# Attention scores of the first two groups from the split parts, 32 rows at a time, and a new order of the first loads and preparations

## The chip, the core and the metric

One core of a Trainium2 chip. A core has five engines with queues of their own: PE (matrix multiplies, into the eight PSUM banks), DVE (vector), ACT (activations), POOL (GpSimd) and SP (used here to issue DMAs). They run side by side and wait for each other by semaphores. The metric is the device time of one execution in microseconds (us), the median of the runs shown.

## What is computed

A transformer block on 2048 rows of 512 numbers: cross attention with a residual, then a layer with a shared feed-forward net and eight experts.

```python
attn = einsum('bhdq,bhdk->bhqk', q, k)          # q = layernorm(x), k = v = ctx, heads of 32 channels
out  = einsum('bhqk,bhdk->bhdq', softmax(s * attn), v)
x = x + out
# on layernorm(x): out = top-2 of 8 experts (gelu, rank-32 side path) + 0.2 * shared net
x = x + moe(layernorm(x))
```

The heads lie along the 128 rows of a group: a group has 4 heads of 32 rows, and 16 groups make 2048 rows. A score matrix of one head is 512 x 512.

## The kernel before

The function `work_order` writes one list of units by hand, `plan`; every engine walks through this list and issues its own part of each unit, in that order. So the place of a unit in the list sets the order on all engines at once, and a wait in one unit holds all that stands behind it on that engine.

Group g goes through these units. **load** g (SP): x rows to `xin` and context rows to `cin` (four and two buffers). **prepare** g: `stats`, `aggr`, `rstd` (layer norm; DVE, with a power of one column on POOL between, L719), `norm` (DVE L1002), `x_hi`, `x_lo`, `c_lo` (DVE L1008, L1012, L1017, and ACT L811 for the context): the normed rows and the context rows, each as a bf16 high part and a bf16 rest, in `split[g % 2]` (four parts). **bounce** g (SP): the four parts go to DRAM (`split_parts`) and come back as stacks `QS` and `KS`: six DMAs, so that one head's three products hi*hi, lo*hi and hi*lo become one contraction over 96 rows. **score** g, i (16 units: head h, 128 query rows t): one matmul of 96 rows and 512 columns (PE L1335) into a PSUM bank, and DVE takes the row maximum (L1038). **parts**, **rows**, **row**: the negative maxima are turned by PE (L1349) and laid by ACT (L830, four copies) into rows 96 and 97 of `QS`; the matching rows of `KS` are set to one by POOL (unit `fills`, L727). **exp** g, i: a matmul of the stacks, 128 rows (PE L1365), and ACT's exponential (L840). **values** g, t, k: four fp32 matmuls side by side in column strips of 32 (PE L1384), once for the sums and once for the values, the latter from `VT`, which `turn_v` makes by turning `cin` (PE L1317, ACT L825). Then `den`, `attn`, `resid` (DVE L1055 to L1064), a second layer norm (`stats2` to `norm2`, with a POOL step `rstd2`, L723), `x2_hi`, `x2_lo`, `turn`, `gate`, `xt_lo`.

Beside this the weights of the shared net come in: `w_load` 0 to 7 (SP L628, 1 MB each), `w_split` n: ACT makes the bf16 high part of a quarter (L856), and POOL subtracts it in four pieces (L743) for the low part. `wd` and `wu` are small side weights.

After the first two groups (window 0) the kernel runs windows of two groups: `open_window(w)` ends the group before, `scores_and_up(w)` mixes the scores of group 2w+1 with the 16 `up` steps of the shared net (12 matmuls of 256 columns each, PE L1428), `exponentials_and_down(w)` mixes the exponentials with the `down` steps. Seven such windows follow window 0, then the routing and the experts. The change touches window 0 and the first two functions of window 1.

In the first stretch the list is: `load` 0 and 1, `small`, `w_load` 0, `prepare` 0 with its bounce, `w_load` 1, `prepare` 1, `fills`, `w_load` 2 to 7, then the 16 scores of group 0, with `load` 2 and 3 placed among them, behind all weight loads on SP's queue.

Of the kernel before, what the change touches and what calls it, by code (L numbers as in the profile page):

```python
# [4 lines left out]

# [9 lines left out]
P = 128  # L15
# [19 lines left out]
STACK = 6  # L35
# [17 lines left out]
def work_order():  # L53
# [98 lines left out]
    def open_window(w):  # L152
# [20 lines left out]
        if w < WINDOWS:  # L173
            add("turn_v", 2 * w + 1)
            add("load", 2 * w + 2) if 2 * w + 2 < GROUPS else None
# [10 lines left out]
        if w < WINDOWS:  # L186
            add("parts", 2 * w)
            if 2 * w + 3 < GROUPS:
                add("load", 2 * w + 3)

    def scores_and_up(w):
        a = 2 * w
        score = scores((a + 1) * UNITS, (a + 2) * UNITS)
        rows = max_rows(a)
        for n, _ in enumerate(shared_up(w - 1)):
            if n >= 3:
                next(rows, None)
            next(score, None)
        for _ in score:
            pass  # L200
        add("parts", a + 1)

    def exponentials_and_down(w):
        downs = [shared_down(w - 1, 0)] if w else []
        for k, g in enumerate((2 * w, 2 * w + 1)):
            score = iter(())
            if k == 1:
                side = [average(g - 1), norm2(g - 1), rows2(g - 1)]
            elif w < WINDOWS - 1:
                side = [prepare(n) for n in (g + 2, g + 3)]  # L210
                if w == 0:
                    score = scores(UNITS, 2 * UNITS)
            else:
                side = []
            values = []
            rows = max_rows(g + 1)
            for i in range(UNITS):
# [4 lines left out]
                if w == 0 and k * UNITS + i in (2, 14, 18, 22, 26):  # L222
                    add("w_split", 3 + (2, 14, 18, 22, 26).index(k * UNITS + i))
                if i >= 4 * k:
                    one_of(side, 3 if k and i < 6 else 2)
# [27 lines left out]
    add("load", 0)  # L253
    add("load", 1)
    add("small")
    add("w_load", 0)
    for _ in prepare(0):
        pass
    add("w_load", 1)
    for _ in prepare(1):  # L260
        pass
    add("fills")
    for k in range(2, 8):
        add("w_load", k)
    add("rank_load")
    add("w_split", 0)
    for i, _ in enumerate(scores(0, UNITS)):
        if i in (0, 4):
            add("turn_v", i // 4)
        if i in (6, 12):  # L270
            add("load", 1 + i // 6)
        if i in (2, 8):
            add("w_split", 1 + i // 8)
    add("scales")
    add("parts", 0)
    for _ in max_rows(0):
        pass
    early, placed = [], []
    exponentials_and_down(0)
    add("wd", E)  # L280
    for w in range(1, WINDOWS):
        open_window(w)
        if w == 1:
            add("b2_parts")
            add("wu", E)
        scores_and_up(w)
# [66 lines left out]
def build(nc, x, ctx_in, itok, gate_w, w1, b1, w2, b2, wd, wu, sw1, sb1, sw2, sb2, swd, swu, out):  # L353
    stack = ExitStack()
    with stack:
# [226 lines left out]
        def sync_program(sp):  # L582
            dma = nc.sync.dma_start
            for unit in plan:
                kind = unit[0]
                if kind == "load":
# [5 lines left out]
                    dma(xin[g % NX][:, :], x_rows[rows, :]).then_inc(s_x[g % NX], 16)  # L592
                    if g >= 2:
# [11 lines left out]
                elif kind == "bounce":  # L605
# [11 lines left out]
                    for dst, parts in ((QS[s], (0, 1, 0)), (KS[s], (2, 2, 3))):  # L617
                        if g == 0 and dst is KS[0]:
                            continue
# [77 lines left out]
        def pool_program(pool):  # L697
# [16 lines left out]
            for unit in plan:  # L714
# [9 lines left out]
                elif kind == "fills":  # L724
                    pool.wait_ge(s_clo, 2)
                    for i in range(NS):
                        gp.memset(KS[i][96:P, :, :], 1.0).then_inc(s_fills, 1)  # L727
                        pool.wait_ge(s_fills, i + 1)
                    gp.memset(wus[96:P, :], 0.0).then_inc(s_fills, 1)
# [4 lines left out]
                elif kind == "w_split":  # L734
                    n = unit[1]
# [6 lines left out]
                    for a in range(4):  # L742
                        gp.tensor_tensor(lo[:, a], whole[:, a], hi[:, a], ALU.subtract).then_inc(s_wlog, 1)  # L743
# [58 lines left out]
        def act_program(act):  # L802
            act.wait_ge(s_pool, CONSTANTS)
            for unit in plan:
                kind = unit[0]
                if kind == "x_hi":
                    g = unit[1]
                    if g >= 2:
                        act.wait_ge(s_stack[(g - 2) % NS], 16 * STACK * ((g - 2) // NS + 1))
                    act.wait_ge(s_c[g % 2], 16 * (g // 2 + 1))  # L810
                    ac.activation(split[g % 2][:, 2, :], cin[g % 2][:, :], ACT.Copy).then_inc(s_khi, 1)  # L811
                elif kind == "bounce" and unit[1] == 0:
                    act.wait_ge(s_parts, 16)
                    for k, which in enumerate((2, 2, 3)):
                        ac.dma_start(KS[0][HD * k:HD * k + HD, :, :],
                                     parts_dram[0, which].rearrange("(h p) c -> p h c", p=HD)).then_inc(s_stack[0], 16)
                elif kind == "fills":
# [152 lines left out]
        def dve_program(dve):  # L970
# [9 lines left out]
            for unit in plan:  # L980
# [22 lines left out]
                elif kind == "x_hi":  # L1003
                    g = unit[1]
                    if g >= 2:
                        dve.wait_ge(s_stack[(g - 2) % NS], 16 * STACK * ((g - 2) // NS + 1))
                    dve.wait_ge(s_dve, chain)
# [10 lines left out]
                elif kind == "fills":  # L1018
# [245 lines left out]
        def pe_program(pe):  # L1264
# [38 lines left out]
            for unit in plan:  # L1303
                kind = unit[0]
                if kind == "fills":
# [13 lines left out]
                elif kind == "score":  # L1319
# [3 lines left out]
                    if i == 0:  # L1323
# [6 lines left out]
                    if was:  # L1330
# [4 lines left out]
                    mm(bank(score_bank[unit]), QS[s][0:96, h, t * P:t * P + P], KS[s][0:96, h, :],  # L1335
                       start=True, stop=True).then_inc(s_score, 1)
# [15 lines left out]
                elif kind == "exp":  # L1352
# [5 lines left out]
                    if i == 0:  # L1358
                        pe.wait_ge(s_row, GH * (g + 1))
# [245 lines left out]
```

## Time and profile before

| | us |
|---|---|
| median of 3 runs (1519.56 to 1521.75) | 1519.76 |
| the profiled execution | 1527.68 |
| its span, first to last instruction | 1525.9 |
| first score matmul | 17.56 |
| rows of maxima of group 0 / group 1 on PE | 31.93 / 67.59 |
| first `rank` matmul (the shared net begins) | 113.75 |
| last `up` matmul of window 1 | 142.6 |
| each later window | 82.61 |

The page's first part gives busy time by engine: PE 1417.7 (93% of the span), DVE 779.3 (51%), ACT 695.8 (46%), POOL 222.0 (15%). Over the whole span PE is the engine that is nearly always busy; the first 100 us are the exception. What a stage is limited by is read from that stage's own rows: which engine sits idle there, and what ended its idle time.

### The profile page before, as it was taken

Reading aid. Unit: us, or ns where it says so; the run is one execution under the profiler, and the core shown is the slowest. Engines: PE = TensorE matmul, PEld = TensorE weight load, DVE = VectorE, ACT = ScalarE, POOL = GpSimd, SP = SyncE. Lnnn points to the kernel's source line nnn. Section 1 sums busy time; section 2 is a strip of 40 time slices with the busy share of each in tenths; the row PEclk is TensorE's granted clock in tenths of the full one; section 3 lists DMA queues with packets and bytes.
Section 4 is the critical chain, followed back from the end, with each engine's and each line's share of the span. In section 5 each row is a group of like instructions: output and inputs, shape, how many; then the busy total and the mean of one; then the engine's idle time right before and its main releaser. Section 6 shows DMA issues by size and latency. Waiting matters only on the chain.

```text
span 1525.9 us, 27002 instructions
## 1 busy us (share of the span) xinstructions
PE 1417.7 (93%) x11297; PEld 1001.1 (66%) x11368; DVE 779.3 (51%) x1287; ACT 695.8 (46%) x1015; POOL 222.0 (15%) x219
## 2 busy tenths in 40 slices
PE   3569999999999999988999999999999999999996
PEld 1126372726354453626588888998888888888884
DVE  5477565756574756726462552625436264352620
ACT  4546456464737373743443434534344343443411
POOL 6240000000000000053300201203021120210202
PEclk8779999999999999999999999999999999999998
DMA  8410213122222212202832543526345262441402
GB/s 271 152 55 15 77 49 90 50 83 56 74 66 70 70 49 56 78 15 29 284 111 85 144 111 113 144 85 178 92 130 128 85 170 85 132 130 65 91 6 35
DMA packets 93211, 145.41 MB, mean 95 GB/s; under 512 B 15529, under 2 KB 36153, under 8 KB 93090
## 3 DMA queue, kind: packets, MB, share of 16 engines
q1 hardware_dynamic: 80370, 118.08, 23.5%
q0 software_dynamic: 12288, 25.21, 9.6%
q8 instruction: 90, 1.47, 0.4%
q10 hardware_dynamic: 432, 0.39, 0.1%
q14 instruction: 31, 0.25, 0.1%
HBM read 109.47 MB, written 34.15 MB: 94 GB/s over the span
## 4 chain that ended last, share of the span: by engine, by line
PE 78%; issue 11%; DVE 4%; ACT 2%; DMA 1%; POOL 1%; SPq 1%; another core or an unknown queue 0%; POOLq 0%; ACTq 0%; DVEq 0%
PE banks L1545 23%; PE banks L1520 23%; PE banks L1428 11%; PE banks L1445 7%; PE banks L1384 3%; PE banks L1335 3%; PE banks L1508 2%; PE banks L1365 1%; PE banks L1482 1%; PE banks L1560 1%; PE banks L1404 1%; DVE rowmax L1038 1%; DMA split_parts<-hidden 1%; DMA xin<-in_x 1%; ACT hidden L840 1%
## 5 line engine op out<-in xcount | busy, mean ns | idle before, releaser
L1545 PE MATMUL banks<-hidden,w2h 128*128 128x0 bf16 x2048 | 324.5, 276 | 0.0
L1545 PEld LDWEIGHTS banks<-hidden,w2h 128*128 128x128 bf16 x2048 | 198.3, 98 | 29.3
L840 ACT ACTIVATE hidden<-banks,scales 128x512 f32<-128x512 f32 x256 | 163.4, 684 | 109.5 <-PE banks L1365 86.7
L1545 PE MATMUL banks<-hidden,w2l 128*128 128x0 bf16 x1024 | 198.5, 275 | 0.0
L1038 DVE TENSOR_REDUCE rowmax<-banks 128x1 f32<-128x512 f32 x256 | 170.4, 680 | 43.8 <-PE banks L1335 43.1
L929 ACT ACTIVATE hf<-banks,b1cols 128x640 f32<-128x640 f32 x128 | 101.5, 793 | 181.5 <-PE banks L1520 178.9
L1445 PE MATMUL banks<-w2h,hidden 128*128 128x512 bf16 x499 | 176.3, 382 | 1.0 <-issue 0.2
L1164 DVE TENSOR_TENSOR w1l<-stage,w1h 128x2048 bf16<-128x2048 f32 x32 | 73.3, 2292 | 193.5 <-ACT w1h L905 193.5
L1335 PE MATMUL banks<-KS,QS 96*128 96x512 bf16 x256 | 100.8, 403 | 38.1 <-DVE rowmax L1038 27.2
L1520 PE MATMUL banks<-eth,w1l 128*128 128x0 bf16 x1024 | 135.9, 276 | 0.0
L1520 PE MATMUL banks<-eth,w1h 128*128 128x0 bf16 x1024 | 135.9, 276 | 0.0
L1520 PE MATMUL banks<-etl,w1h 128*128 128x0 bf16 x1024 | 135.9, 276 | 0.0
L935 ACT ACTIVATE yT<-banks 128x640 f32<-128x640 f32 x32 | 22.5, 703 | 195.9 <-PE banks L1545 195.9
L1365 PEld LDWEIGHTS banks<-QS,KS 128*128 128x128 bf16 x256 | 20.6, 98 | 136.7 <-ACT hidden L840 83.3
L1520 PEld LDWEIGHTS banks<-eth,w1l 128*128 128x128 bf16 x1024 | 99.8, 98 | 15.2
L1545 PEld LDWEIGHTS banks<-hidden,w2l 128*128 128x128 bf16 x1024 | 99.9, 98 | 15.2
L1520 PEld LDWEIGHTS banks<-etl,w1h 128*128 128x128 bf16 x1024 | 99.8, 97 | 15.2
L1365 PE MATMUL banks<-QS,KS 128*128 128x512 bf16 x224 | 81.3, 397 | 30.5 <-ACT hidden L840 18.7
L1520 PEld LDWEIGHTS banks<-eth,w1h 128*128 128x128 bf16 x1024 | 99.9, 98 | 14.7
L1155 DVE CAST hidden<-hf 128x640 bf16<-128x640 f32 x128 | 62.9, 492 | 88.7 <-ACT hf L929 88.5
L1157 DVE TENSOR_TENSOR hidden<-hf,hidden 128x640 bf16<-128x640 f32 x128 | 105.6, 825 | 4.4
L1055 DVE RECIPROCAL rden<-banks 128x128 f32<-128x128 f32 x64 | 55.1, 914 | 95.4 <-PE banks L1384 67.2
(176 smaller groups left out, 2025.5 us busy)
## 6 DMA issues: line engine op xcount, KB each, us to landing
stage<-in_L_ffn_w SPq DMA_DIRECT2D x64, 1024.0 KB
split_parts<-hidden SPq DMA_DIRECT2D x16, 512.0 KB, 3.0
QS<-split_parts SPq DMA_DIRECT2D x48, 128.0 KB, 2.5
KS<-split_parts SPq DMA_DIRECT2D x45, 128.0 KB, 2.7
xin<-in_x SPq DMA_DIRECT2D x16, 256.0 KB, 2.8
cin<-in_ctx SPq DMA_DIRECT2D x16, 256.0 KB, 2.9
out_rows<-xin SPq DMA_DIRECT2D x16, 256.0 KB, 2.0
normed_rows<-x2r SPq DMA_DIRECT2D x16, 256.0 KB, 2.0
```

The lines of the kernel that those rows point to most:

```text
L840: ac.activation(prob[n % NPH], bank(score_bank[unit]), ACT.Exp, scale=scales[:, g // 2:g // 2 + 1]).then_inc(s_exp, 1)
L929: ac.activation(by_half(hf[n % 2][:, :]), PB[:, b0:b0 + 2, 0:CAP].rearrange("p j (c r) -> p j c r", r=HP), ACT.Gelu, bias=b1cols[:, e * FB ...
L1038: dv.reduce_max(rowmax[g % 2][:, i:i + 1], bank(score_bank[unit]), X_AXIS).then_inc(s_max, 1)
L1155: link(dv.tensor_copy(hh[:, fb, :], hf[n % 2][:, :]))
L1157: dv.tensor_tensor(hl[:, fb, :], hf[n % 2][:, :], hh[:, fb, :], ALU.subtract).then_inc(s_hl, 1)
L1164: dv.tensor_tensor(lo, stage[j % NST][:, :].rearrange("p (a w) -> p a w", w=512), hi, ALU.subtract).then_inc(s_wlo, 1)
L1335: mm(bank(score_bank[unit]), QS[s][0:96, h, t * P:t * P + P], KS[s][0:96, h, :], start=True, stop=True).then_inc(s_score, 1)
L1365: mm(bank(score_bank[unit]), KS[s][:, h, t * P:t * P + P], QS[s][:, h, :], start=True, stop=True).then_inc(s_st, 1)
L1428: issued = mm(bank(b)[:, 0:PASS], weights[:, kb, f0:f0 + P], data[:, kb, :], start=n == 1, stop=n == 3 * KB)
L1445: issued = mm(bank(b_down), a[:, fb, cols], w[:, fb, :], start=False, stop=(fb, k) == (FB - 1, 2))
L1520: issued = mm(half_of(bank(b0 + j)).shape_from_register(bank_cols(e, j)), weights[:, kb, f0:f0 + P], half_of(data[:, kb, :], j).shape_from ...
L1545: issued = mm(half_of(bank(b0 + j)).shape_from_register(bank_cols(e, j)), w[:, fb, rows], half_of(a[:, fb, :], j).shape_from_register(slot ...
```

## The change

- Scores of groups 0 and 1 no longer use the stacks. Each is three matmuls of 32 rows (hi*hi, lo*hi, hi*lo) that add up in one bank, read straight from `split[g]` at the head's own rows 32h to 32h+31. They wait for `x_lo` and `c_lo` of the group in place of the six stack DMAs, and run head by head in turn. The stacks are still made, for the exponentials.
- `load` is parted in `load` (x) and `c_load` (context). x 2 and 3 are loaded at the start; context 2 after `w_load` 2, context 3 before `w_load` 5.
- `prepare` 1 stands behind the scores of group 0, `prepare` 3 in the exponentials of group 1. All six stack DMAs of group 0 are on SP (three were on ACT). `split` of groups 2 and 3 may be written only when the scores of groups 0 and 1 are done.
- `w_split` keeps ACT's part; POOL's four pieces are units of their own, `w_lo`, strewn among the following units. `fills` is in two parts: `KS` 0 and 1 early, the rest behind the last piece.
- In window 1, the last eight scores of group 2 move from `open_window` to the first `up` steps; `b2_parts` and `wu` move behind `up` 8. An `exp` waits for its own head's row copy.

```diff
     def scores(first, last):
         for n in range(first, last):
-            add("score", n // UNITS, n % UNITS)
+            g, i = divmod(n, UNITS)
+            add("score", g, i % GH * QT + i // GH if g < 2 else i)
             yield
...
         score = scores(2 * w * UNITS + EARLY, (2 * w + 1) * UNITS) if w < WINDOWS else iter(())
+        late = score if w == 1 else iter(())
+        if w == 1:
+            score = iter(())
...
         for n, _ in enumerate(shared_up(w - 1)):
-            if n >= 3:
+            if n >= (6 if w == 1 else 3):
                 next(rows, None)
             next(score, None)
+            if w == 1 and n < 8:
+                next(score, None)
+            if w == 1 and n == 9:
+                add("b2_parts")
+                add("wu", E)
...
                 side = [average(g - 1), norm2(g - 1), rows2(g - 1)]
+                if w == 0:
+                    side.insert(0, prepare(g + 2))
...
-                if w == 0 and k * UNITS + i in (2, 14, 18, 22, 26):
-                    add("w_split", 3 + (2, 14, 18, 22, 26).index(k * UNITS + i))
+                if w == 0 and k * UNITS + i in (4, 12, 20, 28):
+                    n = 3 + (4, 12, 20, 28).index(k * UNITS + i)
+                    split_quarter(n)
+                else:
+                    low_piece()
...
+    for g in range(2):
+        add("load", g)
+        add("c_load", g)
+    for g in range(2, 4):
+        add("load", g)
     add("small")
     add("w_load", 0)
...
-    add("w_load", 1)
-    for _ in prepare(1):
+    for k in range(1, 3):
+        add("w_load", k)
+    add("c_load", 2)
+    for k in range(3, 5):
+        add("w_load", k)
+    add("turn_v", 0)
+    add("turn_v", 1)
+    for i, _ in enumerate(scores(0, UNITS)):
+        if i == 4:
+            add("fills", 0)
+        if i in (6, 10, 14):
+            split_quarter(i // 4 - 1)
+        else:
+            low_piece()
+    add("parts", 0)
+    rows = max_rows(0)
+    for _ in second:
+        next(rows, None)
+        low_piece()
+    for _ in rows:
         pass
+    add("scales")
+    add("rank_load")
+    add("c_load", 3)
+    for k in range(5, 8):
+        add("w_load", k)
...
-    add("wd", E)
+    split_quarter(7)
+    while pieces:
+        low_piece()
+    add("fills", 1)
...
-                    if i == 0:
+                    if i == 0 and g < 2:
+                        pe.wait_ge(s_xlo, g + 1)
+                        pe.wait_ge(s_clo, g + 1)
+                    elif i == 0:
                         pe.wait_ge(s_stack[s], 16 * STACK * (g // NS + 1))
...
+                    if g < 2:
+
+                        rows = slice(HD * h, HD * h + HD)
+                        for k, (q, c) in enumerate(((0, 2), (1, 2), (0, 3))):
+                            issued = mm(bank(score_bank[unit]), split[g][rows, q, t * P:t * P + P], split[g][rows, c, :],
+                                        start=k == 0, stop=k == 2)
+                        issued.then_inc(s_score, 1)
...
-                    if i == 0:
-                        pe.wait_ge(s_row, GH * (g + 1))
+                    if i == 0 and g < 2:
+                        pe.wait_ge(s_stack[s], 16 * STACK)
+                    if t == 0:
+                        pe.wait_ge(s_row, GH * g + h + 1)
```

PE at the end of the scores of group 0 and the first exponentials. Before (L1335 a score, L1349 the rows, L1365 an exp):

```order
L1335 MATMUL banks<-KS_65,QS_61 128x512 x11
L1349 MATMUL banks<-identb,MS 32x128 x16
L1365 MATMUL banks<-QS_61,KS_65 128x512
L1335 MATMUL banks<-KS_66,QS_62 128x512
L1365 MATMUL banks<-QS_61,KS_65 128x512
```

Now (L1397 a score of 32 rows, L1415 the rows, L1433 an exp):

```order
L1397 MATMUL banks<-hidden 128x512 x2
L1415 MATMUL banks<-identb,MS_74 32x128 [waits s_vtc,s_ms]
L1415 MATMUL banks<-identb,MS_74 32x128 x15
L1433 MATMUL banks<-QS0_61,KS0_65 128x512 [waits s_row,s_max,s_stack0,s_fills]
L1397 MATMUL banks<-hidden 128x512 [waits s_max,s_clo,s_xlo]
L1397 MATMUL banks<-hidden 128x512 x2
L1433 MATMUL banks<-QS0_61,KS0_65 128x512 [waits s_max,s_row]
```

Each matmul of a score has become three of 32 rows, and the first of group 1 waits for `prepare` 1 itself.

POOL from its first power (the layer norm's `rstd`) to the second layer norm of group 1. Before (L719 `rstd`, L727 `fills`, L743 low pieces, L723 `rstd2`):

```order
L719 TENSOR_TENSOR mv<-mv,half 128x1 x2
L727 MEMSET KS_65 32x2048
L743 TENSOR_TENSOR w1l<-w2h,w1h 128x512 x8
L743 TENSOR_TENSOR w1l<-w2l,w1h 128x512 x4
L719 TENSOR_TENSOR mv<-mv,half 128x1
...
L743 TENSOR_TENSOR w2l<-hidden,w2h 128x512 x8
L723 TENSOR_TENSOR mv<-mv,half 128x1
L743 TENSOR_TENSOR w2l<-late_stage,w2h 128x512 x4
L723 TENSOR_TENSOR mv<-mv,half 128x1
```

Now (L773 `rstd`, L781 `fills`, L798 low pieces, L777 `rstd2`):

```order
L773 TENSOR_TENSOR mv<-mv,half 128x1
L781 MEMSET KS_65 32x2048
L781 MEMSET KS_66 32x2048
L798 TENSOR_TENSOR w1l<-w2h,w1h 128x512 x8
L798 TENSOR_TENSOR w1l<-w2l,w1h 128x512
L773 TENSOR_TENSOR mv<-mv,half 128x1
...
L798 TENSOR_TENSOR w2l<-hidden,w2h 128x512 x2
L777 TENSOR_TENSOR mv<-mv,half 128x1
L798 TENSOR_TENSOR w2l<-hidden,w2h 128x512 x6
L798 TENSOR_TENSOR w2l<-late_stage,w2h 128x512 x4
L781 MEMSET KS_67 32x2048
```

The `rstd` of group 1 now stands behind nine low pieces, the `rstd2` of group 0 behind two pieces of its quarters in place of eight, and that of group 1 behind the late `fills`.

SP, the issue of loads around the weights. Before:

```order
L632 DMA wuf<-in_L_ffn_swu 32x512 x3
L592 DMA xin_56<-in_x 128x512
L597 DMA cin_58<-in_ctx 128x512
L592 DMA xin_57<-in_x 128x512
L597 DMA cin_59<-in_ctx 128x512
```

Now:

```order
L653 DMA cin_59<-in_ctx 128x512
L645 DMA xin_56<-in_x 128x512
L645 DMA xin_57<-in_x 128x512
L655 DMA scale_i<-in_itok_B_1933 128x8
...
L682 DMA w2l<-in_L_ffn_sw 128x4x512
L653 DMA cin_58<-in_ctx 128x512
L682 DMA w2l<-in_L_ffn_sw 128x4x512
```

x 2 and 3 (`xin_56`, `xin_57`) have moved from behind all weight loads to the front, and context 2 stands between two of them.

## Rows read from the trace of the kernel before

**Rows 1.** Busy time by stage: us, PE, PEld, DVE, ACT, POOL busy (instructions), PEclk, DMA share, GB/s.

```profile
0.00:17.56 17.56, 0.66 (x2) 0.36 (x3) 6.67 (x15) 5.83 (x6) 6.15 (x17) 1.00 0.77 220
17.56:31.93 14.37, 8.35 (x25) 3.56 (x25) 12.97 (x21) 3.67 (x4) 14.00 (x14) 0.77 0.84 284
31.93:48.75 16.82, 3.94 (x23) 1.09 (x24) 2.20 (x6) 9.81 (x12) 5.46 (x5) 0.60 0.96 329
48.75:67.59 18.84, 15.47 (x71) 3.19 (x73) 16.43 (x28) 9.12 (x13) 6.38 (x6) 0.80 0.33 105
67.59:99.35 31.76, 20.90 (x120) 4.01 (x122) 16.66 (x27) 18.67 (x25) 19.67 (x17) 0.79 0.12 38
99.35:113.75 14.40, 8.37 (x42) 6.41 (x39) 12.35 (x23) 3.67 (x5) 0.66 (x1) 0.66 0.30 95
113.75:142.60 28.85, 28.65 (x238) 23.11 (x237) 21.00 (x43) 16.06 (x35) 0.00 (x0) 0.93 0.03 8
150.17:232.78 82.61, 79.00 (x553) 41.09 (x559) 51.20 (x98) 46.54 (x84) 4.33 (x6) 1.00 0.23 66
```

**Rows 2.** Chain of work that ended last, first 152 us: start, length, what.

```profile
7.78 3.99 DMA split_parts<-hidden
...
39.41 7.77 DMA xin<-in_x
...
77.15 4.52 POOL w2l L743 x4
81.69 4.89 POOL w2l L743 x4
...
122.91 1.31 PE banks L1428 x12
```

**Rows 3.** Timeline, matmuls: start, length of the merged piece, engine, line, operation, count.

```profile
17.96 1.06 PE L1317 MATMUL banks<-ident,cin 128*128 128x128 f32 x4
18.81 1.91 PE L1335 MATMUL banks<-KS,QS 96*128 96x512 bf16 x4
...
61.39 0.38 PE L1335 MATMUL banks<-KS,QS 96*128 96x512 bf16 x1
61.70 1.07 PE L1384 MATMUL banks<-hidden,VT 128*32 128x512 f32 x8
62.70 0.39 PE L1365 MATMUL banks<-QS,KS 128*128 128x512 bf16 x1
...
72.08 1.94 PE L1384 MATMUL banks<-hidden,ones_f 128*32 128x512 f32 x8
...
90.44 0.10 PEld L1335 LDWEIGHTS banks<-KS,QS 96*128 96x128 bf16 x1 [6.32 <-DVE rowmax L1038]
```

**Rows 4.** Timeline of ACT, POOL and SP; in brackets the idle time before and its releaser.

```profile
14.58 7.37 POOL L727 MEMSET KS<- 32x2048 bf16 x4 [5.24 <-DVE hidden L1017]
22.05 1.27 SPq L621 DMA_DIRECT2D QS<-split_parts  x3
23.98 8.93 POOL L743 TENSOR_TENSOR w1l<-w2h,w1h 128x512 bf16<-128x512 f32 x8
31.25 1.91 ACT L856 ACTIVATE w1h<-w2l 128x2048 bf16<-128x2048 f32 x1 [8.18 <-DMA w2l<-in_L_ffn_sw]
33.18 2.42 ACT L830 ACTIVATE QS<-banks 32x512 bf16<-32x512 f32 x4
```

**Rows 5.** Timeline of DVE.

```profile
19.48 9.23 DVE L1038 TENSOR_REDUCE rowmax<-banks 128x1 f32<-128x512 f32 x15 [0.59 <-PE banks L1335]
50.00 0.78 DVE L1002 TENSOR_SCALAR xn<-xin,mv 128x512 f32<-128x512 f32 x1
53.56 1.64 DVE L1017 TENSOR_TENSOR hidden<-cin,hidden 128x512 bf16<-128x512 f32 x1
```

**Rows 6.** Stretches of 1 us, PE alone: us, PE busy (instructions), PEclk, DMA share, GB/s.

```profile
25.00:26.00 1.00, 0.66 (x2) 0.70 1.01 273
52.00:53.00 1.00, 1.00 (x9) 0.65 0.00 0
```

More of the change, by code:

```diff
@@ L4 @@
 from concourse import mybir
+import itertools
 import numpy as np
@@ L185, in open_window, with scores_and_up, late_scores @@
             pass
[L186 removed]
+        if 1 < w < WINDOWS:
             add("parts", 2 * w)
[L188 to L193 removed]
+        if 2 * w + 3 < GROUPS:
+            add("load", 2 * w + 3)
+            add("c_load", 2 * w + 3)
+        return late
+    def scores_and_up(w, late):
+        a = 2 * w
+        def late_scores():
+            for _ in late:
+                yield
+            if w == 1:
+                add("parts", a)
+        score = itertools.chain(late_scores(), scores((a + 1) * UNITS, (a + 2) * UNITS))
         rows = max_rows(a)
         for n, _ in enumerate(shared_up(w - 1)):
[L196 removed]
+            if n >= (6 if w == 1 else 3):
                 next(rows, None)
             next(score, None)
+            if w == 1 and n < 8:
[3 more added lines that the diff above has]
+                add("wu", E)
         for _ in score:
@@ L251, in beside, with split_quarter, low_piece @@
             yield
-    add("load", 0)
-    add("load", 1)
+    pieces = []
+    def split_quarter(n):
+        add("w_split", n)
+        pieces.extend((n, a) for a in range(4))
+    def low_piece():
+        if pieces:
+            add("w_lo", *pieces.pop(0))
+    for g in range(2):
[3 more added lines that the diff above has]
+        add("load", g)
     add("small")
     add("w_load", 0)
-    for _ in prepare(0):
-        pass
-    add("w_load", 1)
-    for _ in prepare(1):
-        pass
-    add("fills")
-    for k in range(2, 8):
+    first, second = prepare(0), prepare(1)
+    for _ in range(8):
+        next(first)
+    add("k_hi", 1)
+    for _ in first:
+        pass
+    for k in range(1, 3):
[18 more added lines that the diff above has]
+    for _ in rows:
+        pass
+    add("scales")
+    add("rank_load")
+    add("c_load", 3)
+    for k in range(5, 8):
         add("w_load", k)
[L265 to L277, printed above, removed]
     early, placed = [], []
     exponentials_and_down(0)
-    add("wd", E)
+    split_quarter(7)
+    while pieces:
+        low_piece()
+    add("fills", 1)
     for w in range(1, WINDOWS):
[L282 to L286, printed above, removed]
+        scores_and_up(w, open_window(w))
         if w == WINDOWS - 1:
@@ L809, in act_program @@
                         act.wait_ge(s_stack[(g - 2) % NS], 16 * STACK * ((g - 2) // NS + 1))
+                    if g in (2, 3):
+                        act.wait_ge(s_score, UNITS * (g - 1))
                     act.wait_ge(s_c[g % 2], 16 * (g // 2 + 1))
                     ac.activation(split[g % 2][:, 2, :], cin[g % 2][:, :], ACT.Copy).then_inc(s_khi, 1)
[L812 to L817, printed above, removed]
+                elif kind == "fills" and unit[1] == 0:
                     act.wait_ge(s_scale, 1)
```

41 lines of the change are left out of this document (25 added, 16 removed).

## The prediction, made before the changed kernel ran

> **What bounds the kernel now.** I read the stages first [rows 1]. From 150 us on each window takes 82.61 us, PE is busy 79.0 of them at the full clock (1.00, 2.4 GHz), and the change leaves all windows after the first up stage as they are. In the up stage (113.75 to 142.6) PE is busy 28.65 of 28.85 us. So the change can win only before 113.75 us, and may lose in the up stage; what has been won at 142.6 us is the result, since the rest only shifts. Before 113.75 us no engine is full. Then I read the chain [rows 2] for what each stage waits for. Up to 17.56 us: the bounce of group 0, whose write starts at 7.78 and lands 3.99 us later, and the stack reads behind it. Up to 31.93: DVE's row maxima, 9.23 us for 15 [rows 5], 0.62 us each, while a score of 512 columns costs PE 0.22 us at the full clock (twelve matmuls of 256 columns take 1.31 us [rows 2]; the 0.38 in other rows is a modelled length). Up to 48.75: x of group 2, issued at 39.41 behind all weights, landing 7.77 us later; PE is busy 3.94 of 16.82 us. From 67.59 to 113.75: PE is busy 29.3 of 46.2 us; the longest hole is 6.32 us before 90.44 [rows 3], where DVE's second layer norm waits for a power on POOL that stands behind eight low pieces (77.15 and 81.69) [rows 2].
>
> **Step 1: the scores of group 0 start early, and it is worth little.** They need only the four parts, ready at 7.78 us. Both turns of V now stand ahead of them on PE (1.06 us each at the low clock [rows 3], with a copy on ACT between), so the first score starts at about 8.5 us instead of 17.56. Sixteen scores of three matmuls at the full clock are 16 x 0.65 = 10.4 us, DVE's maxima 9.8 us, so with some first scores at the low clock (3 x 0.43 = 1.3 us; pace of 1.91 = 3 x 0.43 + 0.63 [rows 3]) they end near 22 us, 7 us earlier than before. But the next score, the first of group 1, waits on PE for `prepare` 1, and that has gone behind them. Nothing of the 7 us is kept unless `prepare` 1 keeps up.
>
> **Step 2: what `prepare` 1 waits for.** Its `rstd` stands on POOL behind nine low pieces, and the ninth needs `w_split` 2, so `w_load` 2. Two more loads of 256 KB stand ahead of the first bounce: 0.52 MB at 284 GB/s [rows 1] would be 1.8 us; part of it falls in a slack of the queue, I take 1.2, so the write lands at 13.0 instead of 11.77. Before, from the issue of a stack's six DMAs (22.05) to the moment ACT could take the 1 MB weight load behind it (31.25) went 9.2 us [rows 4]. So `w_load` 1 is there at 22.2 us, and `w_load` 2 after another 1.05 MB at 329 GB/s [rows 1], at 25.4. ACT splits each in 1.91 us [rows 4]: 24.1 and 27.3. POOL takes 1.12 us a piece (8.93 for eight): four pieces of quarter 1 end at 28.6, the ninth at 29.7, and with 0.6 allowed for the power of one column DVE goes on at 30.3. That is from `norm` to `c_lo`. Before, for group 2 and beside a busy POOL, that took from 50.00 to 55.20 with two maxima between [rows 5]: 5.2 - 1.24 = 3.9 us. So `c_lo` 1 is ready at 34.2 us. The four row copies of ACT (2.42 [rows 4]) end at about 30 us and are hidden by this; if `prepare` 1 came earlier, they would bound it.
>
> **Step 3: exponentials of group 0 beside scores of group 1.** x of group 2 is long there, so the hole of 7.77 us [rows 2] is gone. But PE now has per pair of exp and score 0.22 + 3 x 0.22 = 0.87 us instead of 0.43, and each pair goes from 128 rows to 32 and back. No row shows such a switch; the nearest is that to column strips: from a score's start to the strips' start 0.31 us instead of 0.22, and from there to the next exp 1.00 us for four passes of 0.22 [rows 3], so 0.09 + 0.14 = 0.23 us for there and back. I take 0.23 from this row; the bounds are 0 and 0.43 (a matmul's whole time, twice). A pair is 1.10 us, sixteen 17.6; five steps of values lie between, 1.09 us each, 5.5. The stage starts at the low clock, as it did at 48.75, where the rise came between 52 and 53 us [rows 1, 6]; the same again loses 2 us. Sum 25.1 us: the last score ends at 59.3. DVE's 16 maxima and one preparation (9.9 + 3.9 us) and ACT's work (9.12 us in this stage before, with a split of 1.91 and an exponential or two more now) lie beside it. Then come one maximum (0.62), the last values step (1.09) and the parts: I allow 1.8 us, so the rows of maxima come at 61.1 instead of 67.59. **Won so far: 6.5 us.**
>
> By the Trainium skill (page TensorEngine Tiling (Array Packing), Key Properties) changing the tiling mode drains TensorE, which speaks against interleaving these two forms. The rows above show the same for column strips, 0.23 us for there and back; by a change without any drain the sum of the stage would be 3.7 us less.
>
> **Step 4: from the rows of group 1 to the shared net (46.2 us before).** Gone: the hole of 6.32 us [rows 3], as the power of group 0 stands behind two pieces now; and five maxima of group 2 between 99.35 and 113.75, where DVE is busy 12.35 of 14.4 us [rows 1], 5 x 0.62 = 3.1. Added: `prepare` 3 on DVE (3.9 us as in step 2, and its statistics), hidden, since DVE idles here (16.66 busy of 31.76 [rows 1]) until the values of group 0 are summed; without this cover it would cost them whole. Part of the hole comes back: POOL's pieces ended at 86.58 [rows 2], so 3.9 us of it, up to 90.44, were DVE's own second norm and casts beside POOL, which stay; one maximum now stands ahead of the casts, so I take 2.7 (bounds 0 and 3.9). New: `fills` and all low pieces stand ahead of the last power (group 1) on POOL: eight pieces of 1.12 from when ACT has split quarter 6, then two memsets of 1.84 (7.37 for four) and the rest of `fills`, 2.0 (from 21.95 to 23.98) [rows 4]; that ends some 4 us after DVE asks for the power, and `norm2`, `turn`, `gate` and the first `rank` are queued behind it. Sum -6.3 - 3.1 + 2.7 + 4.0 = -2.7. **Won so far: 9.2 us**, `rank` at about 104.5 us. The bounds of the POOL wait are 0 (ACT reaches the splits earlier) and 8 (it reaches them 4 us later).
>
> **Step 5: the up stage gets longer.** Before, an up step took 1.31 us [rows 2] and a score of 0.22. Now the first eight steps carry two scores: 0.22 x 8 = 1.8 us more for PE. DVE was busy 21.0 of 28.85 us in this stage [rows 1]; eight maxima more are 5.0 us, all in its first half, which makes 10.5 + 5.0 us of work in 14.4: DVE becomes the bound there, and PE's next scores wait for maxima that stand behind a step's rest. `b2_parts` and `wu` only move within the stage. Bounds: 1.8 (PE alone) and 5.0 (all eight maxima on the path); I take 3.3, between them, as both engines are near their limit. **Sum: -6.5 - 2.7 + 3.3 = -5.9 us.** The profiled execution would go from 1527.68 to about 1521.8; the median by the same shift from 1519.76 to **1513.9 us** (0.4%).
>
> **The rivals.** *The slower side: the clock.* Before, the granted clock fell between 25 and 26 us while PE still worked (0.66 of that us) and rose between 52 and 53 [rows 6]. If it stays low through the stretches with 32-row matmuls, both score stages run at 1.2 GHz: group 0 ends at about 30 us instead of 22, which puts `prepare` 1 some 3 us later, and a pair costs 0.43 + 1.28 + 0.23 = 1.94 us, so 31.0, and the values 5 x 1.94 [rows 3] = 9.7: 40.7 instead of 25.1. Then -5.9 + 15.6 + 3 = +12.7: 1532.5 us. It decides from about 6 us of low clock lost. For it: a score stage with gaps lost the clock. Against it: PE has no gaps here. *No change: `prepare` 1 comes late.* Every us of `w_load` 2 is one of the end. Were it as late as the same load before (31.25), the sum would be -5.9 + 5.8 = 0: 1519.7. For it: nine pieces on POOL and two splits in a row. Against: there it stood behind the bounce of group 1, which now stands behind it. *Also near no change: the weights of a 32-row matmul load in the open.* Before, loads hide behind the matmul ahead. 48 loads of some 0.1 us [rows 3] make +4.8: 1518.7. By the Trainium skill (TensorE: Matmul & The Clock Gate, The mechanism) a weight load overlaps only with matmuls of another row group, and the three of one score are of one group; before, no row could show it. *More: no switch cost and POOL in time.* -5.9 - 3.7 - 4.0 = -13.6: 1506.2.
>
> **How the numbers follow.** A change of 0.2% (3.0 us) is about what a measurement of this kernel can tell from none. Forecast (gain of 3 to 10 us) 0.5; more than that 0.15; no change by a late `prepare` 1 or open weight loads 0.2; the clock 0.15. Faster 0.65, same 0.19, slower 0.16. The forecast's own range is 1510 to 1517. The range goes from the case of more, 1505, to open loads with the dearer up stage (-5.9 + 4.8 + 1.7, and 2 us for the bounds of step 2), 1523; the clock's case is left out.
>
> **What the profile will show.** Right, if: the first 32-row matmul starts near 8.5 us and the scores of group 0 end near 22; then PE idles until `c_lo` 1 near 34; the rows of group 1 come near 61, the first `rank` near 104 after a wait of DVE's norm for POOL, and the last `up` near 136.5; the windows stay at 82.6. Wrong, if the clock is low through 35 to 60 us, a pair of exp and score takes over 1.3 us at the full clock, or `prepare` 1 ends outside 31 to 38 us.

## The result and the profile after

The changed kernel takes 1529.91 us (median of 4, 1529.06 to 1532.23) where the kernel before took 1520.76 beside it: 1.0071 times as long, 95% interval 1.0048 to 1.0095. It is slower by 0.7%; the prediction had said 0.4% faster. The profiled execution took 1532.23 us, its span is 1530.4.

The stages of the changed kernel, in the columns of [rows 1]:

```profile
0.00:8.67 8.67, 2.10 (x8) 1.43 (x8) 3.30 (x7) 3.03 (x4) 3.52 (x15) 1.00 0.72 228
8.67:21.43 12.76, 10.38 (x53) 3.31 (x52) 10.31 (x20) 3.89 (x4) 7.24 (x6) 1.00 0.73 233
21.43:38.26 16.83, 0.61 (x16) 0.48 (x18) 5.68 (x9) 6.17 (x6) 9.82 (x9) 1.00 0.56 211
38.26:79.57 41.31, 40.84 (x111) 7.17 (x115) 15.97 (x28) 16.15 (x20) 9.97 (x9) 1.00 0.47 153
79.57:122.87 43.30, 26.20 (x154) 8.81 (x149) 28.80 (x50) 21.73 (x29) 20.89 (x20) 0.80 0.23 73
122.87:157.70 34.83, 31.55 (x245) 23.06 (x246) 24.53 (x50) 16.11 (x36) 0.00 (x0) 0.95 0.03 10
165.30:247.90 82.60, 78.88 (x552) 41.06 (x558) 51.21 (x98) 46.59 (x83) 4.23 (x7) 1.00 0.23 64
```

The cuts are the first score, the rows of group 0, the first score of group 1, the rows of group 1, the first `rank` matmul, the last `up`, and a later window. The first score of group 0 is 8.9 us earlier than before and its rows are 10.5 us earlier; 21.43 is the last mark that is early. Then PE idles 16.2 us; then the exponentials of group 0 and the scores of group 1 take 41.3 us, of which PE is busy 40.84. The rows of group 1 come at 79.57 instead of 67.59, `rank` at 122.87 instead of 114.18 (its first matmul; the table's 113.75 is the weight load in front of it), the last `up` ends at 157.7 instead of 142.6. From there on both kernels run windows of 82.6 us, 15.1 us apart.

What PE does in the scores of group 0, in the 41.3 us, and (last line) behind them (timeline: start, length of the merged piece, engine, line, operation, count):

```profile
8.67 1.48 PE L1397 MATMUL banks<-hidden 32*128 32x512 bf16 x12
14.96 5.04 PE L1397 MATMUL banks<-hidden 32*128 32x512 bf16 x21 [0.19 <-DVE rowmax L1093]
38.26 1.43 PE L1397 MATMUL banks<-hidden 32*128 32x512 bf16 x3 [16.22 <-DVE hidden L1072]
39.63 0.61 PE L1433 MATMUL banks<-QS,KS 128*128 128x512 bf16 x1
40.17 1.46 PE L1397 MATMUL banks<-hidden 32*128 32x512 bf16 x3
41.56 0.61 PE L1433 MATMUL banks<-QS,KS 128*128 128x512 bf16 x1
49.26 1.94 PE L1452 MATMUL banks<-hidden,ones_f 128*32 128x512 f32 x8
84.89 1.12 PE L1452 MATMUL banks<-hidden,VT 128*32 128x512 f32 x8
```

From exp to exp 39.63 to 41.56, 1.93 us, and so on to the end of the stage; a values step 1.94, as in the row at 72.08 of [rows 3] (1.07 in the row at 61.70). These are the lengths of 1.2 GHz; the first values step at 2.4 GHz, 1.12, comes at 84.89, behind the rows of group 1. The clock column says 1.00 all the while, and it cannot be read here: in this trace it shows no other value before 95 us, while the same exponential takes 0.61 us here and 0.38 in the stretches of [rows 3] at 2.4 GHz. So in this stage the level is read from the durations. By the Trainium skill (TensorE: Matmul & The Clock Gate, Part 1: The HAM clock gate) clock events in a trace have been seen to be unreliable; this trace agrees.

The chain of waits (start, length, what):

```profile
7.85 6.30 DMA split_parts<-hidden
16.92 8.26 DMA w2h<-in_L_ffn_sw
27.19 5.59 POOL w1l L798 x5
103.28 8.98 POOL w2l L798 x8
112.31 1.81 POOL KS L781
118.16 0.56 POOL mv L777
128.60 1.33 PE banks L1496 x12
131.33 1.21 DVE rowmax L1093 x2
132.98 1.33 PE banks L1496 x12
147.33 0.69 DVE b2f L1085
153.27 1.31 PE banks L1496 x12
154.80 1.31 PE banks L1496 x12
```

Up to 38 us it is the bounce's write, the second weight load and POOL's pieces. Then it is PE alone (the pairs above), then POOL ahead of the last power. In the up stage two maxima stand in every second step, and later `b2_parts`.

**Why 15.1 us in the marks are 9.2 in the medians.** The executions of the kernel before lie further apart (1513.8 to 1526.2 in 29 of them) than those of the changed kernel (1527.9 to 1532.2 in 10). A second profile of the kernel before shows where two of them differ:

> The kernel before, profiled a second time. In the first profile ACT stood 5.0 us at 663.77 us without a visible cause, and the way from 645.8 us to the first up matmul behind it (706.61) took 60.8 us against 50.3 in the changed kernel. If this belongs to one execution only: about 50 us here, and the profiled time near 1521. If it belongs to the kernel: about 60 us again.

It took 1514.9 us. Its first `rank` and last `up` are those of the first profile (114.03 and 142.49). From 645.8 us to the third `up` step behind it, which the expectation calls the first, went 49.7 us (to 695.54), in the first profile 60.8 (to 706.61). The first profile's chain has there, on ACT:

```profile
663.77 4.98 another core or an unknown queue
```

So 11 of the 12.8 us between the two lie in a stage that the change does not touch. The 1514.9 us are near the lowest of the 29 executions; that most of the others carry some of this time fits, but only these two were profiled. Against 1514.9 the medians of the changed kernel (1529.91, and 1529.39 in experiment 5) are 15.0 and 14.5 us longer, near the 15.1 and 12.8 us of its marks. What stops ACT there, and why the changed kernel shows less of it, was not found.

### The profile page after: what moved, and what is told of

Read it like the earlier page. It is cut to its first block, busy times and chain, and to the rows that moved or that the text cites. A ratio compares the mean times of both kernels' runs of the same rounds, so it can differ in the third digit from the quotient of the medians.

```text
span 1530.4 us, 27182 instructions
## 1 busy us (share of the span) xinstructions
PE 1439.3 (94%) x11361; PEld 1003.2 (66%) x11432; DVE 779.8 (51%) x1287; ACT 697.5 (46%) x1015; POOL 221.9 (14%) x219
## 3 DMA queue, kind: packets, MB, share of 16 engines
q0 software_dynamic: 12288, 25.21, 9.6%
## 4 chain that ended last, share of the span: by engine, by line
PE 74%; issue 12%; DVE 4%; POOL 3%; ACT 3%; DMA 2%; SPq 0%; POOLq 0%; ACTq 0%
PE banks L1613 23%; PE banks L1588 23%; PE banks L1496 9%; PE banks L1513 5%; PE banks L1401 3%; PE banks L1452 3%; PE banks L1576 2%; PE banks L1397 1%; POOL slot_table L824 1%; PE banks L1628 1%; PE banks L1433 1%; PE banks L1550 1%; DMA stage<-in_L_ffn_w 1%; PE banks L1472 1%; PE banks L1483 1%
## 5 line engine op out<-in xcount | busy, mean ns | idle before, releaser
L1433 PEld LDWEIGHTS banks<-QS,KS 128*128 128x128 bf16 x256 | 20.4, 98 | 141.4 <-issue 79.6
L1433 PE MATMUL banks<-QS,KS 128*128 128x512 bf16 x224 | 82.4, 404 | 20.4 <-ACT hidden L892 13.4
L1401 PE MATMUL banks<-KS,QS 96*128 96x512 bf16 x224 | 85.6, 388 | 13.2 <-DVE rowmax L1093 11.5
L926 ACT ACTIVATE hf<-banks,sb1cols 128x256 f32<-128x256 f32 x128 | 60.6, 474 | 77.1 <-PE banks L1496 72.6
```

Of the source, the lines that this page charges most:

```text
L1433: mm(bank(score_bank[unit]), KS[s][:, h, t * P:t * P + P], QS[s][:, h, :], start=True, stop=True).then_inc(s_st, 1)
```

## The experiments

The runs were made in three groups, each on one chip with the kernel before beside it: `tall`, `one32`, `up_back`, `before_again` (kernel before 1519.87 us); `rows64`, `hybrid`, `hybrid_f`, `one32_ubf` (1530.54); `after_again`, `b2_back`, `hybrid_32`, `hybrid_again` (1520.10). Across groups only ratios and marks are compared.

**1. Is it the height of the matmuls?** The scores of group 1 over all 128 rows, everything else equal:

```
-                        rows = slice(HD * h, HD * h + HD)
+                        rows = slice(HD * h, HD * h + HD) if g == 0 else slice(0, P)
```

> The changed kernel, but the three matmuls of a score of group 1 read all 128 rows of the split parts instead of the head's own 32 (so the row maxima of group 1 are those of four heads summed, and only shift the exponent of the softmax; the exponentials themselves are as before). Count, columns, order and waits are the same. Theory A (32-row matmuls leave the clock at 1.2 GHz): the clock rises within a few us of 38 us, a pair of exp and score falls from 1.92 to about 0.87 us, a values step from 1.87 to 1.00; the stage takes 16 x 0.87 + 5 x 1.0 + 2 = 21 us instead of 41.3, and the median falls from 1529.9 to about 1510. Theory B (the clock stays low because PE idled from 22 to 38 us before the stage, or because each pair changes the tile form): as the changed kernel where it is the idle time, 1529.9; B's second half would agree with A here.

Measured: 1512.64 us, ratio 0.9957 (0.9941 to 0.9974). The timeline of PE in this run:

```profile
35.39 1.44 PE L1397 MATMUL banks<-hidden 128*128 128x512 bf16 x3 [12.49 <-DVE hidden L1072]
38.75 1.49 PE L1397 MATMUL banks<-hidden 128*128 128x512 bf16 x3
40.03 0.63 PE L1433 MATMUL banks<-QS,KS 128*128 128x512 bf16 x1
40.46 0.87 PE L1397 MATMUL banks<-hidden 128*128 128x512 bf16 x3
41.17 0.38 PE L1433 MATMUL banks<-QS,KS 128*128 128x512 bf16 x1
41.38 0.81 PE L1397 MATMUL banks<-hidden 128*128 128x512 bf16 x3
42.03 0.38 PE L1433 MATMUL banks<-QS,KS 128*128 128x512 bf16 x1
60.57 0.41 PE L1415 MATMUL banks<-identb,MS 128*32 128x128 bf16 x16 [1.90 <-DVE MS L1102]
```

The stage begins at 35.39; at 40.46, 5.1 us later, the exponential falls from 0.63 to 0.38 us and a pair from 1.71 to 0.87. The rows of group 1 come 25.2 us after the stage's start (41.3 in the changed kernel). The number of matmuls, columns and waits is the same. Of these 16 us at most 3.5 are the change of form between 32 and 128 rows, which this run removes as well (1.93 us a pair against 1.71 at 1.2 GHz, sixteen times); the rest is the clock.

**2. Fewer of them.** One 32-row matmul a score of group 1 instead of three:

```
-                        for k, (q, c) in enumerate(((0, 2), (1, 2), (0, 3))):
+                        for k, (q, c) in enumerate(((0, 2),) if g == 1 else ((0, 2), (1, 2), (0, 3))):
```

> The changed kernel, but a score of group 1 is one matmul of 32 rows (hi*hi alone) instead of three; its row maxima lack the two small products and only shift the exponent. One third of the 32-row matmuls is left, each still beside an exp of 128 rows, with the same switch of form. Theory A, if any 32-row matmul in the mix keeps the clock down: pair 0.43 + 0.43 + switch, about 0.95 us, values 1.87, the stage 16 x 0.95 + 5 x 1.87 = 24.6 us, median about 1513. If what counts is the share of full-height matmuls (A'): the clock rises, pair about 0.5 us, stage about 15 to 17 us, median about 1505. Theory B (idle before the stage): low clock throughout, 24.6 us.

1514.02 us, ratio 0.9969 (0.9949 to 0.9989). PE in the middle of the stage:

```profile
52.85 0.60 PE L1397 MATMUL banks<-hidden 32*128 32x512 bf16 x1
53.38 0.61 PE L1433 MATMUL banks<-QS,KS 128*128 128x512 bf16 x1
53.92 0.60 PE L1397 MATMUL banks<-hidden 32*128 32x512 bf16 x1
```

In this execution a pair takes 1.07 us and the clock stays at 1.2 GHz from 35.96 to 64.39, 28.4 us instead of 41.3; it rose at 69.64, 7 us after the last 32-row matmul (in the changed kernel too, where the scores go on to 77.9 and the rise is at 84.89). But the profile of `one32_ubf` (experiment 6), with the same stage, has the other outcome, from 45.1 us on:

```profile
47.05 0.39 PE L1427 MATMUL banks<-QS,KS 128*128 128x512 bf16 x1
47.37 0.38 PE L1391 MATMUL banks<-hidden 32*128 32x512 bf16 x1
47.69 0.39 PE L1427 MATMUL banks<-QS,KS 128*128 128x512 bf16 x1
```

A pair of 0.64 us, 2.4 GHz, and the stage is over after 21.8 us. So with one 32-row matmul beside each of 128 rows it goes either way. With three beside each it did not in any of five profiles (the changed kernel twice, `up_back`, `b2_back`, `hybrid_32`): 41.3 us each time.

**3. Height or the change of form?** 64 rows, which alternate with 128 as 32 do:

```
-                        rows = slice(HD * h, HD * h + HD)
+                        rows = slice(HD * h, HD * h + HD) if g == 0 else slice(0, 64)
```

> The changed kernel, but the matmuls of a score of group 1 read 64 rows of the split parts, so 64 rows lie between the 32 of the change and the 128 of the run before (row maxima of two heads summed; they only shift the exponent). Theory A, the height of the matmuls sets the clock: either it rises within some us of the stage's start (pair about 0.87 us) or it stays at 1.2 GHz (pair about 1.7 to 1.9 us); this run shows on which side 64 rows lie. Theory C, the change of tile form between a partial and a full-height matmul keeps the clock down, not the height: low throughout, pair 1.9 us, since the form changes as often as with 32 rows.

```profile
37.04 1.44 PE L1397 MATMUL banks<-hidden 64*128 64x512 bf16 x3 [15.08 <-DVE hidden L1072]
44.75 1.46 PE L1397 MATMUL banks<-hidden 64*128 64x512 bf16 x3
46.14 0.61 PE L1433 MATMUL banks<-QS,KS 128*128 128x512 bf16 x1
50.48 0.89 PE L1397 MATMUL banks<-hidden 64*128 64x512 bf16 x3
56.51 0.39 PE L1433 MATMUL banks<-QS,KS 128*128 128x512 bf16 x1
56.84 0.82 PE L1397 MATMUL banks<-hidden 64*128 64x512 bf16 x3
57.59 0.39 PE L1433 MATMUL banks<-QS,KS 128*128 128x512 bf16 x1
67.28 0.41 PE L1415 MATMUL banks<-identb,MS 128*32 128x128 bf16 x16 [1.28 <-DVE MS L1102]
```

The clock rose at 50.48, 13.4 us after the stage's start at 37.04: between the 5.1 us of 128 rows and never in 41.3 us with 32. So the change of form alone does not hold it down (theory C falls): the form changes as often as with 32 rows, and the rows of group 1 come 30.2 us after the start instead of 41.3. Only the height differs between the three. That 64 rows rise later than 128 rests on one profile each, and experiment 2 shows that the moment can differ between executions. The form has a price of its own: a pair at 2.4 GHz is 1.08 us here (56.51 to 57.59) and 0.87 with 128 rows, 0.21 us for there and back; with 32 rows it is 0.20 (0.64 above, less two passes of 0.22). (One execution, 1532.06 us beside 1530.54 for the kernel before; no ratio is taken from it.)

**4. Or the 16 us of idle PE ahead of the stage?** `hybrid` keeps the early scores of group 0 in 32 rows, but takes those of group 1 from the stacks, with `prepare` 1 and its bounce ahead of the scores of group 0 and window 1 as before. The later splits of the weight quarters move with it (not all shown):

```
-                    if g < 2:
+                    if g < 1:
...
     for _ in first:
         pass
+    for _ in second:
+        pass
...
-        if i in (6, 10, 14):
-            split_quarter(i // 4 - 1)
+        if i == 6:
+            split_quarter(0)
```

`hybrid_32` differs from `hybrid` in one thing, 32-row scores for group 1 again (`if g < 2:`, and the wait that goes with it).

> Scores of group 0 early from the split parts, 32 rows, as in the changed kernel; but scores of group 1 from the stacks (one matmul of 96 rows), prepare 1 with its bounce ahead of the scores of group 0 as in the kernel before, splits of weight quarters 1 and 2 behind the row copies, and window 1 as before. Theory A: the clock rises in the stage of exponentials, which takes about 18 us as before (18.8) instead of 41.3; it starts when stack 1 is there, about 31 us; rows of group 1 near 50 us, first rank near 95 us, median about 1501, 19 us below before. Rival: the weights now come behind two bounces and POOL's low pieces end late, so that the norm of group 0 or rank waits for them and half of it is lost: rank near 104, median 1510.

> As hybrid, but the scores of group 1 are three matmuls of 32 rows each again; nothing else differs. Theory A: the clock stays at 1.2 GHz over the stage of exponentials: 16 pairs at 1.92 us and five values steps at 1.87, 40 us from its start near 25 us, rows of group 1 near 66 us instead of 49.9, first rank near 112 instead of 96.5, median 16 us above hybrid. If the low clock of the changed kernel came from the idle time ahead of that stage (16 us, here 1.3 us): the clock rises, the stage takes about 25 us, within 3 us of hybrid.

> hybrid once more, on the chip of hybrid_32 and of the changed kernel: the marks as in the first run (rows of group 1 at 49.9, first rank at 96.5), the median 17 to 20 us below the kernel before.

On one chip `hybrid_32` took 1514.76 us, ratio 0.9972 (0.9956 to 0.9988), and `hybrid` 1499.34, ratio 0.9871 (0.9840 to 0.9902); in the second group `hybrid` stood at 0.9873 (0.9837 to 0.9909). The stage from the first score of group 1 to the rows of group 1, first `hybrid_32`, then `hybrid` on the same chip:

```profile
24.90:66.23 41.33, 40.86 (x111) 7.18 (x115) 16.87 (x26) 18.89 (x23) 13.98 (x12) 1.00 0.66 228
```

```profile
25.01:48.35 23.34, 16.25 (x79) 3.53 (x81) 17.12 (x26) 17.85 (x23) 12.88 (x12) 1.00 1.02 364
```

In `hybrid_32` PE idles for no more than 2 us at a time between the first score of group 0 and the stage, and the stage takes 41.33 us as in the changed kernel; in `tall` PE idled 12.5 us ahead of it and the clock rose. So it isn't the idle time. Scores of 32 rows for group 1 cost 18 us in the marks and 15.4 in the median; this holds, beside the clock, the two more matmuls a score and the change of form. `hybrid` beats both kernels: its first `rank` is at 94.98 us, its last `up` ends at 123.66, 19 us ahead of the kernel before. The early scores of group 0 and the early x 2 and 3 let the stage begin at 25 us instead of 48.75 [rows 1], and with its 96-row scores the clock rose within it, in all three profiles of `hybrid` and `hybrid_f`.

**5. The up stage.** `up_back` undoes the edits to window 1 (late scores, start of the rows, `b2_parts` and `wu`), with `b2_parts` and `wu` ahead of the up stage; `b2_back` does only the latter:

```
-            if w == 1 and n == 9:
-                add("b2_parts")
-                add("wu", E)
...
-        scores_and_up(w, open_window(w))
+        late = open_window(w)
+        if w == 1:
+            add("b2_parts")
+            add("wu", E)
+        scores_and_up(w, late)
```

> The changed kernel with its edits to window 1 undone: the last eight scores of group 2 stand in open_window again, the rows start behind up 2, b2_parts and wu stand ahead of the up stage. If the up stage is 6.0 us longer because of the eight late scores and b2_parts/wu, it falls back from 34.8 to about 28.9 us; the stage from the rows of group 1 to the first rank gets 3.1 us longer (five maxima at 0.62). Net -2.9: about 1527.0. Rival: the late scores were hidden in the up stage and its length comes from the low clock or from another order, net within 1 us of 1529.9.

> The changed kernel with only b2_parts and wu put back ahead of the up stage; the eight late scores stay in it. The up stage took 34.8 us in the changed kernel and 28.4 where both were put back. If the two units on the chain (3.3 us there) make up half of it: about 31.5 us, and the time 3 us less than the changed kernel. If it is the maxima of the late scores alone: 34.5 us, no change.

`up_back` took 1524.91 us, ratio 1.0041 (1.0024 to 1.0058); `b2_back` 1529.57, 1.0073 (1.0047 to 1.0100), beside a second run of the changed kernel:

> The changed kernel a second time, beside the kernel before on the same chip. Its marks at 142 to 214 us stand 15.1 us behind those of the kernel before, but the first medians differ by 9.2 us only. If the other 6 us belong to the executions of the kernel before (time in its last window that comes and goes, up to 12 us between two profiles), the marks differ by 15 us again and the median by 9 to 15.

That took 1529.39, 1.0071 (1.0046 to 1.0095); its marks stand 12.8 us behind those before at the last `up` (155.32), 2.3 less than in its first profile, because its second weight load came 2.7 us earlier. First `rank` to last `up`, `up_back`, then `b2_back`:

```profile
123.09:151.49 28.40, 28.00 (x237) 22.79 (x236) 20.81 (x43) 16.08 (x35) 0.00 (x0) 0.95 0.03 12
```

```profile
122.04:155.25 33.21, 31.61 (x245) 23.23 (x246) 24.66 (x50) 16.09 (x35) 0.00 (x0) 0.94 0.03 10
```

Of 34.8 us in the changed kernel (in both profiles) `b2_parts` and `wu` are 1.6, the late scores 4.8; the rest is the 28.4 of before. The 1.6 do not show in the median of `b2_back` (1529.57 against 1529.39); in its profile the stage of exponentials began 1.3 us later than in that of `after_again`. That the late scores shorten the way to `rank` came out smaller: from the rows of group 1 to `rank` 44.7 us with them put back, 43.3 to 43.8 in the changed kernel and `b2_back`, 0.9 to 1.4 and not 3.1. (In `tall`, `one32` and `rows64`, with the same work there, this way took 42.2 to 44.0, so a difference of 1 us in it is near what profiles can tell.)

**6. The late fills.** Behind POOL's power of group 1 instead of ahead of it, with `hybrid` and with `one32` plus `up_back`:

```
+        if w == 1:
+            add("fills", 1)
         if w < WINDOWS:
             add("turn_v", 2 * w + 1)
...
-    add("fills", 1)
...
-                    pool.wait_ge(s_wlog, 32) if unit[1] else pool.wait_ge(s_clo, 1)
+                    pool.wait_ge(s_rstd2, 2) if unit[1] else pool.wait_ge(s_clo, 1)
```

> The changed kernel with one matmul of 32 rows for a score of group 1 (as one32), window 1 as before (as up_back) and the late fills behind the power of group 1. If the three add up: one32 1514.0, less 6 us for the up stage, less 3 to 4 for the fills: about 1505. If the fills cost nothing (low pieces ahead of them are what the power waits for): about 1508.

> As hybrid, and the late fills on POOL stand behind the power of the second layer norm of group 1 instead of ahead of it. If the wait of 4 us of that power in the changed kernel is those fills (two memsets of 1.84 us and the rest): the first rank comes 3 to 4 us earlier than in hybrid and the median falls by as much. If it is the low pieces ahead of them, 0 to 1 us.

`one32_ubf` took 1518.91 us, ratio 0.9937 (0.9915 to 0.9959), 5 us better than `one32`'s, not 9. In the marks it ends its up stage 13 us ahead of `one32` (129.32, 142.32): 6.3 are the rise of the clock, 4.8 window 1 and 1.9 the move of the fills and what else differs on the way to `rank` (rows of group 1 to `rank` 42.8 us, with `up_back` alone 44.7). Why the medians show less is not settled; `one32`'s executions lie in two heaps (five at 1511.8 to 1512.7, five at 1515.4 to 1520.8), as they would if the clock rose in half of them. POOL there:

```profile
85.15 4.50 POOL L792 TENSOR_TENSOR w2l<-late_stage,w2h 128x512 bf16<-128x512 f32 x4
93.72 0.66 POOL L771 TENSOR_TENSOR mv<-mv,half 128x1 f32<-128x1 f32 x1 [4.07 <-DVE mv L1044]
```

The power now waits for DVE, and no longer the other way round. `hybrid_f` took 1510.69 us, 0.9876 (0.9839 to 0.9914), against `hybrid`'s 0.9873: no difference; rows to `rank` 46.3 against 46.7. In both kernels in which the fills were moved the scores of group 2 stand where they stood before, and there DVE's norm waits only 1.19 us for POOL (`up_back`, `hybrid`; 3.63 in the changed kernel). So 0.4 and 1.9 us, one pair of profiles each and within the spread of experiment 5, are what the move was worth there; with the late scores of the changed kernel it was not tried.

## Why the prediction was wrong

**Step 1 held in its marks.** First 32-row matmul at 8.67 us (8.5 said), scores of group 0 done at 20.0 (22 said). But it took the full clock for most of them, and they ran at the low one. What it did not have made up for this: scores of four heads ran beside each other, twelve matmuls in 1.48 us at 1.2 GHz, so that DVE's maxima set the pace even so.

**Step 2 was 4.0 us short, 3.0 of it in its DMA terms.** The write of the bounce took 6.30 us where 5.2 was taken, 5.4 to 6.7 in eight profiles with this order; the second weight load came at 25.21, not 22.2 (22.3 to 25.2 in those profiles). From the load to `c_lo` 1 it is 13.0 us, 12.0 said: DVE's norm to `c_lo` took 4.8 (33.34 to 38.16), not 3.9. Over the profiles the first score of group 1 lies between 35.4 and 38.3, always behind 34.2. Against the 3.99 us of before the write took 1.4 to 2.7 us more, where 1.2 were allowed for the loads ahead of it; that these loads are the whole reason is not shown.

**Step 3 failed, at one term.** The pair was priced at 1.10 us for 2.4 GHz, with 0.23 for the change of form; at that clock it is 1.08 with 64 rows, and the form 0.20 to 0.21 with 32 or 64. By the Trainium skill (TensorEngine Tiling (Array Packing), Key Properties) a change of tiling mode drains TensorE; the 0.21 us agree with that. But the step put the rise of the clock 4 us into the stage, as at 48.75 us before [rows 6], and in that stage all matmuls had 96 or 128 rows. With 32 rows it never came: 41.3 us instead of 25.1 (and 1.8 up to the rows, which lie inside the 41.3). `tall` gives 16 us back by the height, at most 3.5 of them through the form. The rival of the clock had this stage, 40.7 us. Its 1532.5 us in all lie close to the 1529.9 measured partly by luck: its 3 us for late scores of group 0 did not come (done at 20.0, not 30), while 4.0 us in step 2 and 3.1 in step 5 came that it did not have, and the median shows less than the marks. It got a chance of 0.15 because "PE has no gaps here". PE had none, 40.84 of 41.31 us busy, and that did not help: [rows 6] show a clock that fell with gaps, but no row of before shows what a gapless stretch of low matmuls does, and the argument took the one for the other. The Trainium skill (TensorE: Matmul & The Clock Gate, Part 1: The HAM clock gate) says that activity releases the throttle of the clock; in the 41 us here it did not, and the measurement decides. Why low matmuls keep the clock down was not found. The rival of weight loads in the open is out: from the first of three matmuls to the exponential go 1.39 us with 32 rows (40.17 to 41.56) and 1.28 with 128 (38.75 to 40.03), and the 0.11 between them are half of the form's price.

**Step 4 held in its sum, not in its terms.** 43.3 us against 46.6 before, -3.3, said -2.7. The wait for POOL is there (DVE 3.63 us, 4.0 said), but it is not worth its length: with the fills moved the way to `rank` got 0.4 and 1.9 us shorter, and only in kernels whose wait was 1.19. The five maxima were worth 0.9 to 1.4, not 3.1. With them put back (`up_back`) the norm's wait for POOL shrinks to 1.19 us, so this wait covers most of them (DVE, changed kernel, then `up_back`):

```profile
118.74 0.55 DVE L1125 TENSOR_SCALAR x<-xin,mv 128x512 f32<-128x512 f32 x1 [3.63 <-POOL mv L777]
118.15 0.55 DVE L1118 TENSOR_SCALAR x<-xin,mv 128x512 f32<-128x512 f32 x1 [1.19 <-POOL mv L770]
```

**Step 5 was sized too low.** +6.4 instead of +3.3, and outside its bounds (1.8 to 5.0). The late maxima cost 4.8, the end of the range at which each lies on the path: two `up` steps with four scores take 4.38 us (128.60 to 132.98), against 1.53 for one of the last steps (153.27 to 154.80), so 0.66 us more per step, the time of a maximum. And `b2_parts` and `wu`, "only moved", cost 1.6: before, DVE did them while PE did `rank` and the first `up`; behind `up` 8 nothing covers them (the chain at 147.33).

**The sum.** In the marks: rows of group 1 +12.0 instead of -6.5, then -3.3, then +6.4: +15.1 instead of -5.9. Of the 21 us between, 4.0 are step 2, 14.4 step 3, 3.1 step 5, less 0.6 in step 4.

## What to carry to other kernels

Price a stage of 32-row matmuls at the low clock until a trace of one shows otherwise, even when PE would be busy without a gap. Such early scores paid here where PE waited anyway (group 0), not in a stage that PE sets (group 1). Before work is called "moved", name what covered it in its old place and look whether that stands in the new one too. And where a kernel's own executions spread by 12 us, marks in two profiles tell more than two medians.

## What the runs showed of the hardware

- In a stage of the same 64 matmuls (48 of the scores, 16 exponentials) and the values steps between them the clock rose 5.1 us after the start with 128 rows in the scores (one profile), 13.4 us with 64 (one profile), and not within 41.3 us with 32 (five profiles). PE was busy 99% of that time or more (`tall`, `rows64`, the changed kernel).
- Scores of four heads, in four groups of 32 rows, overlapped: twelve matmuls of 512 columns in 1.48 us at 1.2 GHz, where three of one head alone take 1.43 to 1.46.
- With one 32-row matmul to each of 128 rows the clock rose in one execution 8.8 us after the stage's start, and in another not within 28.4 us.
- A change between 64 (or 32) and 128 rows and back costs 0.21 (0.20) us a pair at 2.4 GHz, and 0.22 between 32 and 128 at 1.2 GHz (1.93 us against 1.71).
- The clock column of a profile may show 1.00 where every matmul has the length of 1.2 GHz; the length of one known matmul tells.
